# Position convolutions of a fused vision block: from four 64x64 tiles of the matmul array to sixteen 32x32 tiles

## What is computed

```python
# block L0: attention in 8x8 windows, then a gated 3x3 convolution
qkv = xw @ qkv_w.T + qkv_b                                  # 4 heads of 12
attn = softmax(q @ k.T / sqrt(d) + bias)
x = x + proj(attn @ v)
h = einsum(x, w1_w) + w1_b
g = a * sigmoid(b)                                          # halves of h
y = conv3x3(rep_pad1(g), w2_w) + w2_b                       # full 3x3 convolution
x = x + where(y >= 0, y, 0.2 * y)

# block L1: linear attention between two depthwise position convolutions
x = x + dwconv(x, cpe1_w, cpe1_b)                           # job d0
y = ln2d(x, norm1_w, norm1_b)
act_res = silu(conv1x1(y, act_proj_w, act_proj_b))
t = silu(dwconv(conv1x1(y, in_proj_w, in_proj_b), dwc_w, dwc_b))
q, k = elu(t @ qk_w.T + qk_b) + 1; v = t                    # then rope, kv, z
attn = linear_attention(q, k, v) + dwconv(v, lepe_w, lepe_b)
x = x + conv1x1(attn * act_res, out_proj_w, out_proj_b)
x = x + dwconv(x, cpe2_w, cpe2_b)                           # job d3
y = ln2d(x, norm2_w, norm2_b)
x = x + conv1x1(gelu(conv1x1(y, fc1_w, fc1_b)), fc2_w, fc2_b)
```

## Time and profile before

| | |
|---|---|
| median of 3 runs | 797.29 us (794.84 to 800.06) |
| profiled execution | 800.78 us, its span 799.0 us |
| mean granted clock of TensorE | 0.891 of full speed |
| PE busy | 684.9 us of 799.0 |
| DVE, ACT, POOL busy | 528.7, 432.6, 316.6 us |
| DMA | 20.57 MB in 19473 packets |

### The profile page before, as it was taken

One profiled execution on the slowest core, in us unless ns is written; L12 is line 12 of the kernel. 1 busy time (PEld: TensorE's weight loads), 2 busy tenths in 40 slices (PEclk: granted clock), 3 DMA queues, 4 the chain that ended last, 5 costly groups with the idle time before them and its releaser, 6 DMA issues.

```text
span 799.0 us, 21754 instructions
## 1 busy us (share of the span) xinstructions
PE 684.9 (86%) x9580; PEld 380.8 (48%) x9580; DVE 528.7 (66%) x575; ACT 432.6 (54%) x523; POOL 316.6 (40%) x200
## 2 busy tenths in 40 slices
PE   5899999799899999879889999959887994756795
PEld 4565545456644455446744445536333441542331
DVE  6666418999999144689898411798993117898702
ACT  2588348756565388573352476855413774612334
POOL 8432221348784111235883210037870000487400
PEclk9999999989889999986869989978899997575899
DMA  4200121000010112100100022100000211000001
GB/s 97 58 19 17 48 76 47 17 2 18 2 32 2 34 49 61 42 2 2 32 1 2 16 62 60 33 1 3 1 2 1 63 45 30 2 1 1 1 2 46
DMA packets 19473, 20.57 MB, mean 26 GB/s; under 512 B 8785, under 2 KB 18129, under 8 KB 19379
## 3 DMA queue, kind: packets, MB, share of 16 engines
q1 hardware_dynamic: 17810, 18.95, 9.0%
q10 hardware_dynamic: 1568, 0.22, 0.2%
HBM read 8.39 MB, written 3.54 MB: 15 GB/s over the span
## 4 chain that ended last, share of the span: by engine, by line
PE 30%; DVE 13%; issue 5%; ACT 5%; POOL 3%; DMA 1%; SPq 0%; ACTq 0%; DVEq 0%
PE ps L658 13%; PE ps L648 6%; DVE CT L1258 5%; DVE QS L1244 4%; PE ps L902 2%; PE ps L811 2%; PE ps L884 2%; PE ps L639 1%; ACT L942 1%; PE ps L846 1%; PE ps L821 1%; POOL QH L1387 1%; PE ps L736 1%; PE ps L723 1%; ACT LV L1046 1%
## 5 line engine op out<-in xcount | busy, mean ns | idle before, releaser
L1400 POOL TENSOR_TENSOR SC<-SC,mx 128x768 f32<-128x768 f32 x48 | 80.6, 1680 | 214.2 <-DVE mx L1200 214.0
L1258 DVE SCALAR_TENSOR_TENSOR CT<-TP,vec_sb,CT 112x768 f32<-112x768 f32 x96 | 151.1, 1591 | 0.9
L658 PE MATMUL ps<-ZP,wdw 48*64 48x384 f32 x1728 | 147.2, 491 | 2.4 <-issue 1.4
L658 PEld LDWEIGHTS ps<-ZP,wdw 48*64 48x64 f32 x1728 | 73.4, 135 | 72.8 <-issue 38.1
L1244 DVE SCALAR_TENSOR_TENSOR QS<-ZP,vec_sb,QS 112x768 f32<-112x768 f32 x96 | 107.2, 1160 | 0.3
L1196 DVE TENSOR_TENSOR SC<-ps,bias_sb 128x768 f32<-128x768 f32 x48 | 45.8, 954 | 75.7 <-PE ps L723 43.5
L658 PE MATMUL ps<-G,w_sb 48*64 48x384 f32 x864 | 79.0, 520 | 0.1
L1230 DVE TENSOR_TENSOR LV<-LV,XB 112x768 f32<-112x768 f32 x24 | 24.4, 1017 | 77.9 <-ACT LV L1048 77.9
L942 ACT ACT_TABLE_LOAD x58 | 74.4, 1283 | 1.0
L1371 POOL TENSOR_TENSOR KC<-KK,rope_th_sb 98x384 f32<-98x384 f32 x12 | 17.6, 1466 | 98.6 <-DVE KK L1264 98.5
L658 PEld LDWEIGHTS ps<-G,w_sb 48*64 48x64 f32 x864 | 35.2, 144 | 42.8 <-issue 40.6
(11 more groups left out here) (166 smaller groups left out, 1249.9 us busy)
## 6 DMA issues: line engine op xcount, KB each, us to landing
ZP<-YF SPq DMA_DIRECT2D x48, 75.0 KB, 2.2
XR<-in_x_dram SPq DMA_DIRECT2D x24, 144.0 KB, 2.9
X1T<-in_x_dram SPq DMA_DIRECT2D x24, 144.0 KB, 3.0
XA<-XB SPq DMA_DIRECT2D x48, 72.0 KB, 2.2
out_dram<-XB SPq DMA_DIRECT2D x24, 144.0 KB, 2.3
rope_th_sb<-in_rope_th_dram SPq DMA_DIRECT2D x1, 441.0 KB
w_sb<-in_w_dram SPq DMA_DIRECT2D x2, 81.0 KB, 3.3
wfc_sb<-in_wfc_dram SPq DMA_DIRECT2D x4, 36.0 KB
```

The costliest lines, as they stand in the source:

```text
L658: mm = pe.matmul(slot(job)[half(c, HALF), r * BANK:r * BANK + SPX], w[half(r), tap * HALF:(tap + 1) * HALF], shifted(t, d * CROWS + c * WI ...
L1258: dve.scalar_tensor_tensor(out=ct, in0=win, scalar=wt, in1=ct, op0=ALU.mult, op1=ALU.add).then_inc(lepe_step, 1)
L1400: pool.tensor_tensor(sc, sc, bc_last(mx[:, (q % NSC) * 12:(q % NSC) * 12 + 12], TOK), ALU.subtract).then_inc(sub_ready, 1)
```

## The change

`d0` and `d3` (24 jobs) go from `conv` to a new `conv_quarters`. A chunk's 16 rows are cut into four quarters of 4 rows (192 pixels), and the 48 channels of an image into 32 and 16. Sixteen 32x32 tiles of the array are used: the row group is (image b, channel part g), the column group is the quarter q. A job takes two slots (part g in slot g, image b in bank b) and 144 matmuls of 192 columns in place of 36 of 384. `cv` keeps `conv`.

The result stands with quarters in the partitions. `x3` and `x4` now read both slots with two activations (128 partitions, 2x192 elements) into a new buffer `XQ` (two of them), with biases from a new `quarter_b`. New SP jobs `xq` and `xr` issue eight DMAs each, `XQ` into `XB`. What read `XB` from `x3`/`x4` now waits for these DMAs (`xb_placed`): `xc`, `xc2`, `yn`, `yn2` and `pa`. `XA` becomes two buffers of a chunk, so `pa` waits for `op` two chunks back; the ring `PT` shrinks from six to five. The setup job `s2` has 16 more one-column matmuls and one DVE copy. All five orders are new. In the new `SP_ORDER`, the stretch around `d3` of pair 2 and `d0` of pair 3 reads

The core of the diff (orders left out):

```diff
-NPT = 6
+NPT = 5
+QUARTERS, QPX = 4, CPX // 4
+        quarter_b = sb("quarter_b", [128, 4])
+        XQ = [sb(f"XQ{j}", [128, CPX])[:, :] for j in range(2)]
-        XA = sb("XA", [RG, PX])
+        XA = [sb(f"XA{j}", [RG, CPX])[:, :] for j in range(2)]
...
+                elif name in ("xq", "xr"):
+                    x = ("x3" if name == "xq" else "x4", i, n)
+                    wait_read(sp, ("d0" if name == "xq" else "d3", i, n))
+                    if i and name == "xq":
+                        sp.wait_ge(stored[n], 32 * i)
+                    src = XQ[XQ_COUNT[x] % 2].rearrange("p (g b n) -> p g b n", g=2, b=2)
+                    for q in range(QUARTERS):
+                        p, at = q // 2, n * CPX + (q % 2) * QPX
+                        for g in range(2):
+                            rows = min(QUAD, C - g * QUAD)
+                            dst = XB[p * HALF + g * QUAD:p * HALF + g * QUAD + rows, n * CPX:(n + 1) * CPX]
+                            sp.dma_start(pairs(dst)[:, :, (q % 2) * QPX:(q % 2 + 1) * QPX],
+                                         src[q * QUAD:q * QUAD + rows, g]).then_inc(xb_placed[n], 16)
                 elif name == "pa":
-                    wait_read(sp, ("d0", i, n))
-                    if i:
-                        wait_read(sp, ("op", i - 1, n))
+                    sp.wait_ge(xb_placed[n], 256 * i + 128)
+                    old = before(i, n, 2)
+                    if old:
+                        wait_read(sp, ("op",) + old)
...
+            def conv_quarters(job, w, t, d):
+
+                wait_slot(pe, job)
+                for tap in range(9):
+                    for q in range(QUARTERS):
+                        for g in range(2):
+                            for b in range(2):
+                                rows = slice(b * HALF + g * QUAD, min(b * HALF + (g + 1) * QUAD, RG))
+                                at = tap * HALF + g * QUAD
+                                mm = pe.matmul(slot(job, g)[q * QUAD:(q + 1) * QUAD, b * BANK:b * BANK + QPX],
+                                               w[rows, at:at + QUAD],
+                                               shifted(t, d * CROWS + q * 4, 4, tap)[rows],
+                                               start=(tap == 0), stop=(tap == 8))
+                            if tap == 8 and q == QUARTERS - 1:
+                                mm.then_inc(fill(job, g), 1)
...
-                    conv(job, wdw0, ZP, n)
+                    conv_quarters(job, wdw0, ZP, n)
                 elif name == "d3":
                     wait_read(pe, ("op", i, halo_last(n)))
-                    conv(job, wdw3, ZP, n)
+                    conv_quarters(job, wdw3, ZP, n)
                 elif name in ("xc", "xc2"):
-                    wait_read(pe, ("d0" if name == "xc" else "d3", i, n))
+                    pe.wait_ge(xb_placed[n], 256 * i + (128 if name == "xc" else 256))
...
-                elif name == "x3":
...
+                elif name in ("x3", "x4"):
+                    job = ("d0" if name == "x3" else "d3", i, n)
                     wait_filled(act, job)
+                    j = XQ_COUNT[name, i, n]
+                    if j >= 2:
+                        old = [t for t in XQ_COUNT if XQ_COUNT[t] == j - 2][0]
+                        act.wait_ge(xb_placed[old[2]], 256 * old[1] + (128 if old[0] == "x3" else 256))
+                    dst = XQ[j % 2].rearrange("p (g b n) -> p g b n", g=2, b=2)
+                    for g in range(2):
+                        src = slot(job, g)[:, :].rearrange("p (b n) -> p b n", b=2)[:, :, 0:QPX]
+                        at = (0 if name == "x3" else 2) + g
+                        act.activation(dst[:, g], src, ACT.Identity, bias=quarter_b[:, at:at + 1])\
+                           .then_inc(free(job, g), 2)
```

More of the change, by code:

```diff
@@ L180 @@
+    xq.3.0 st.2.1 xq.3.1 st.2.2 xq.3.2 pa.3.1 pa.3.0 pa.3.2 xr.3.0 xr.3.1 xr.3.2 st.3.1 st.3.0 st.3.2
 """
@@ L195, in places @@
         if "@" in t:
-            token, k = t.split("@")
+            token, ks = t.split("@")
             name, i, n = token.split(".")
-            place[name, int(i), int(n)] = (int(k), uses[int(k)])
-            uses[int(k)] += 1
+            place[name, int(i), int(n)] = []
+            for k in ks.split("+"):
+                place[name, int(i), int(n)].append((int(k), uses[int(k)]))
+                uses[int(k)] += 1
     return place
@@ L255 @@
 TABLE = table_plan(ACT_ORDER)
+XQ_COUNT = {t: j for j, t in enumerate(t for t in jobs(ACT_ORDER) if t[0] in ('x3', 'x4'))}
+QUARTERS, QPX = 4, CPX // 4
 def build(nc, x, wsq, wproj, w2, wfc1, wfc2, vec, fc1b, kbrow, bias, const, ident, masks, rope_y, rope_x,
@@ L366, in build @@
         xa_placed = [sem(f"xa_placed{d}") for d in range(CH)]
+        xb_placed = [sem(f"xb_placed{d}") for d in range(CH)]
         stored = [sem(f"stored{d}") for d in range(CH)]
@@ L680, in run @@
                     pe.matmul(slot(job)[0:RG, 1:2], wq("inp"), v("n1b"), start=True, stop=True)
+                    for j, bias_of in enumerate(("cpe1_b", "cpe2_b")):
+                        for g in range(2):
+                            for q in range(QUARTERS):
+                                pe.matmul(slot(job)[q * QUAD:(q + 1) * QUAD, 2 + 2 * j + g:3 + 2 * j + g],
+                                          eye2_sb[0:C, g * QUAD:(g + 1) * QUAD], v(bias_of)[0:C], start=True, stop=True)
                     for m in range(FG):
@@ L1159, in run @@
                     dve.tensor_tensor(inp_b2, slot(job)[0:RG, 1:2], v("inp_b"), ALU.add)
+                    dve.tensor_copy(quarter_b[:, :], slot(job)[:, 2:6])
                     dve.tensor_tensor(fc1b2[:, :], slot(job)[:, BANK:BANK + FG], fc1b_sb[:, :], ALU.add)
@@ L1261, in run @@
                     job = ("kt", i, n)
-                    k, use = PLACE[job]
+                    k, use = PLACE[job][0]
                     dve.wait_ge(freed[k], 2 * use + 1)
@@ L1350, in _ @@
             op_.then_inc(setup_pool, 1)
-            pool.memset(XA[:, :], 0.0)
+            for t in XA:
+                pool.memset(t, 0.0)
+            pool.memset(XB[:, :], 0.0)
             pool.memset(ZP[:, :, :], 0.0)
```

250 lines of the change are left out of this document (122 added, 128 removed).

## The result

| | before | after |
|---|---|---|
| median, us | 796.42 (794.84 to 800.06, 4 runs) | 877.00 (871.23 to 884.39, 4 runs) |
| profiled execution's span, us | 799.0 | 877.4 |
| mean granted clock of TensorE | 0.891 | 0.870 |

The ratio is 1.0993, 95% interval 1.092 to 1.1065: the change makes the kernel 10% slower. I had predicted 768 us and a range of 740 to 804.

A forecast was written before the change was run, and what follows sets the result against it. PE was taken to bound five stretches where DVE is nearly idle. Gains of 3 + 20 + 8 - 1 = 30 us off 800.8 gave 770.8, scaled 767; forecast 768 us, range 740 to 804.

The forecast's parts named there:

- What bounds: Five PE stretches, PE busy 76 to 99%, DVE nearly idle, count for the convolutions; DVE's stretches stay as they are.
- The convolution's pace: `d0` and `d3`: 11.3 ns a record, a pass 0.165 us, a job 3.25 us against 6.04, 67 us saved over 24 jobs.
- rival 1: Tiles run together but records follow at `av`'s 17.2 ns; a job takes 4.95 us, kernel about 793 us; chance 0.10.
- The instructions at nothing: PE's instruction supply: 0.66 MB more, 40 more blocks, costed at nothing, covered by blocks that come while PE waits.
- break-even: `d0` and `d3`: 288 records a job equal the busy time of before at 21.3 ns a record, 6.13 us a job.
- rival 2: Sixteen tiles don't run together, or records no faster than 29.4 ns; a job 8.5 us, kernel about 845; chance 0.07.
- The hop: `xq`/`xr` on SP: eight issues at 0.52 us, 4.2 us a job (3.2 to 5.1), landing 2.2 us, at most 3.8.
- rival 3: SP's queue takes PE's place: 0.64 us an issue, landings nearer 3.8 us, stretches not shorter; about 802 us; chance 0.11.
- the middle stretches: 256 to 336 and 436 to 516 us: next pair's L0 can cover DMA latency; 10 us gained each, 20 together.
- The end: 755 to 799 us: nothing fills the DMA latency; `xr.3.2` lands at 776, 1.4 us later; 1 us lost.
- ACT's half: `x3` and `x4`: two activations of 0.51 us for one of 0.90, 0.12 us more a job, 3 us over 24, mostly hidden.
- rival 4: Window work covers every DMA; 19 jobs x 2.8 us return, less 1 at the end: 747 us (745 scaled); chance 0.12.

The follow-up runs named there:

- on TensorE alone: Kernel of matmul sections only, nothing of the reference computed; 1024 records on four 64x64 tiles with 64, 96, 112, 128 columns took 28.0, 29.2, 31.3, 30.5 us.
- the cut in four: Kernel before the change, each matmul of `d0` and `d3` cut into four, 288 records a job: 841.68 us, 1.059 of the kernel before.
- the hop without small tiles: Changed kernel with its orders, slots and eight copies a job, but `d0` and `d3` in four 64x64 tiles: 837.12 us, 1.052 of the kernel before.

## Why the prediction was wrong

**What bounds.** Right: the change is felt in the PE stretches and only there (+80.2 us against -1.8 in DVE's).

**The convolution's pace.** The tiles run together, as assumed. The mis-sized term is the pace inside: I took 11.3 ns a record from the columns of four tiles; with sixteen a record costs 15.6 ns at full clock, and with half of the columns still 11.9, so columns count but something comes on top of them. Which part is the records', the weight loads' or the tiles', no run parts. The pace alone would give 288 x 15.6 ns + 0.3 = 4.8 us a job, near rival 1's 4.95.

**The instructions at nothing.** This is the step that failed. I wrote that the 40 more blocks are "covered by blocks that come while PE waits; if it is not, it shows as rival 1's pace". The size was at hand and I didn't use it: a job asks for 2.25 blocks in 3.25 us. The blocks come one at a time, every 3.5 to 4.0 us when PE asks for them at full speed, so 28.5 ns a record (24.6 us / 864), a job of 8.2 us, above my break-even of 21.3. That is rival 2 in its number (29.4 ns, 8.5 us, 845 us) with another mechanism. Its price by the runs: 5.9%, about 47 us, on the kernel before. Blocks that had come while PE waited help only at the start of a run, with one to three blocks (185 records from 89.76 on in the changed kernel; on TensorE alone, with the same tiles and columns, 223 and 351 at 25 and 22 ns a record, during which more may have come).

The Trainium skill, "Runtime: NRT & Kernel Launch", section "Instruction fetch mechanics", states that instructions are refilled in 16 KiB blocks of 256 and that crossing a boundary is mostly hidden. The traces agree on the block and its size. On the hiding they agree for slow records (no break on TensorE alone from 128 columns on) and not for quick ones: 1.1 to 1.7 us at each boundary in the first three jobs of this change. The Trainium skill, "TensorE: Matmul & The Clock Gate", section "Wait — 56ns, not 53.3ns?", with its floor of 25 ns a matmul, spoke against the change, and I had set it aside with `av`'s 14 ns. Inside a burst the measurements keep me right (11.9 to 15.7 ns); over a job they come out near that number (28.5 ns), for a reason that this section doesn't give.

**The hop.** The mechanism was named, rival 3, and the size was off. An issue takes 0.64 us, the upper bound; I had taken 0.52 and let the middle stretches hide most. Measured, the six copies above two cost 26 us in the changed kernel and 41 with a quick convolution (the row of PE's wait for `XB`: 38.0 us). 802 us is what rival 3 said for a quick PE behind this queue, and 802 is what the kernel with three taps took; as that kernel also ran at a lower clock, the match is partly luck. Which wait I had misjudged is known in part: of the 18.7 us that PE waits for `XB` in the changed kernel, 6.4 lie in one wait before 822.0, as the last stretch begins, 4.8 in stretch 3, 1.8 in stretch 4, 1.3 in the last and 0.3 in stretch 2, the rest in DVE's stretches. Of the 25.5 us of stretch 2 the cut in four shows 11.0; the hop without small tiles costs 17.7 there, by a way that stays open.

**The end.** Both `d3` jobs took from 827.6 to 843.7, 16.1 us against 11.7, and the stretch is 10.2 us longer, where I had 1.

**The rest of the sum.** With 96 records and 1.3 us of issues a job the kernel took 761 us, and the stretches 7.0, 7.6, 10.7, 10.2 and 3.6 us less than before, where I had 3, 10, 10, 8 and -1. That is close to the 768 forecast. It is not the forecast's own case, though: its issues were 4.2 us a job, and with 41 us for 3.8 us of issues a job that is about 31 us more, 792. So by this estimate even at PE's predicted pace the change would have brought next to nothing. ACT's half took 577 ns, not 510, so a job cost 0.25 us more instead of 0.12; no stretch shows it. Two slips in the prediction's arithmetic change nothing: the job's terms add to 3.23 us, not 3.25, and rival 4's to 749 us, not 747.

## What to carry to other kernels

Before splitting matmuls into smaller tiles, divide the time of the stretch by the records it will hold: here every run went on at 27 to 31 ns a record (one block of 256 instructions every 3.45 to 4.0 us) once its first one to four blocks were used up, with four, eight and sixteen tiles alike, unless its own pace was slower, and 144 records in 6 us were nearly free where 288 were not. Count a DMA hop by its issues on the queue (0.64 us each) and look in the trace at the work behind them: what the faster engine gains, it may then spend waiting for that queue. Two such prices in one stretch can hide each other in part, so price each with the other removed. And before two paces are compared, read the granted clock of both stretches.

## What the runs showed of the hardware that I had not expected

Narrower records went with a lower granted clock, and the job took no longer for it. Busy time by stretch of the changed kernel, in the `d0` jobs of the first pair:

```profile
89.00:104.00 15.00, 10.26 (x573) 7.82 (x566) 2.12 (x3) 5.95 (x9) 3.06 (x3) 1.00 0.24 61
104.00:118.00 14.00, 10.02 (x381) 6.47 (x375) 1.14 (x2) 3.98 (x7) 0.00 (x0) 1.00 0.15 34
```

and with 96 columns a record:

```profile
89.00:104.00 15.00, 9.89 (x590) 8.02 (x580) 2.11 (x3) 5.95 (x9) 3.05 (x3) 0.68 0.25 62
104.00:118.00 14.00, 9.78 (x317) 6.65 (x318) 0.90 (x2) 2.92 (x5) 0.00 (x0) 0.50 0.15 32
```

The clock, the last column but two, falls from 1.00 to 0.50, that is from 2.4 to 1.2 GHz, after PE has run bursts of narrow records with breaks between them. Each record then costs more (15.9 ns for 11.9), but the burst still ends before the next block is there, so the job doesn't lengthen. It is the work behind that would pay (the whole kernel had a mean clock of 0.785 against 0.870). Narrow records aren't needed for it: the kernel with six of nine taps, with its full 192 columns, fell to 0.50 as its bursts of `d0` ended (0.61 in the mean of the stretch),

```profile
104.00:118.00 14.00, 12.04 (x144) 6.00 (x127) 3.92 (x5) 6.15 (x8) 1.39 (x1) 0.61 0.27 64
```

and the matmuls of `xc` behind them took 1.56 us where they take 0.88 at full clock. On TensorE alone the section of sixteen tiles with 64 columns ran at 0.50 throughout, with 12.9 ns a record, and four 64x64 tiles with 64 columns kept 1.00 with the same breaks. Why the distance of two bursts changes between 3.45 and 4.0 us is open; the block's own packet takes between 0.9 and 1.4 us, which is a part of it.
